# Latents stage rebuilt and run on into the context stage, expert stage's back transposes moved into the first products, row statistics and small attention and last-layer edits

## What is computed

```python
x = x + xattn(ctx_1024, layernorm(x), ...)   # 8192 context rows, 8 heads of 64
x = x + layers(layernorm(x), ...)            # 8 layers: q, k, v, linear attention, MLP 512-2048-512
x = x + experts(layernorm(x), ...)           # 16 experts x 4 sets of 64
```

## Time and profile before

| | us |
|---|---|
| median of 3 runs | 2241.94 |
| lowest and highest | 2238.9, 2242.02 |
| profiled execution | 2242.18 |
| its span in the trace | 2240.4 |

### The profile page before, as it was taken

The page is one execution under the profiler, slowest core; times in us unless marked ns, Lnnn a source line. Parts: engine busy times, 40 slices in busy tenths (PEclk is TensorE's granted clock), DMA queues, the critical chain, the costliest instruction groups (busy, mean ns, idle before and its releaser), DMA issues. The chain is left out here.

```text
span 2240.4 us, 37583 instructions
## 1 busy us (share of the span) xinstructions
PE 2144.8 (96%) x12843; PEld 1082.3 (48%) x12843; DVE 1612.3 (72%) x2356; ACT 1103.8 (49%) x1726; POOL 902.5 (40%) x634
## 2 busy tenths in 40 slices
PE   5899999999999999999899999999999999999976
PEld 2344444433333333333475665757566575756533
DVE  6687777659989999887575757667585666657563
ACT  4122332334444444555464655656474565647445
POOL 0235555559989999600221303122130212213044
PEclk9999999999999999999999999999999999999989
DMA  3345454433322322432323333342333334233313
GB/s 116 130 162 168 167 201 163 148 117 90 93 85 86 97 84 85 124 105 71 125 95 110 98 122 85 132 123 89 114 93 130 85 132 123 81 118 95 116 40 112
DMA packets 159854, 252.75 MB, mean 113 GB/s; under 512 B 11506, under 2 KB 63986, under 8 KB 159730
## 3 DMA queue, kind: packets, MB, share of 16 engines
q1 hardware_dynamic: 159730, 250.96, 35.4%
HBM read 211.73 MB, written 36.70 MB: 111 GB/s over the span
## 5 line engine op out<-in xcount | busy, mean ns | idle before, releaser
L67 PE MATMUL scores<-xt_hi,wt_hi 128*128 128x256 f16 (+3 forms) x1568 | 413.2, 275 | 10.2 <-DVE xt_lo L1418 4.6
L68 PE MATMUL scores<-xt_lo,wt_hi 128*128 128x256 bf16 (+3 forms) x1568 | 413.5, 275 | 0.0
L69 PE MATMUL scores<-xt_hi,wt_lo 128*128 128x256 f16 (+3 forms) x1568 | 413.0, 275 | 0.0
L1375 POOL TENSOR_TENSOR l_rstd<-l_var_eps,neg_half 128x1 f32<-128x1 f32 x71 | 66.6, 938 | 834.6 <-DVE l_var_eps L1429 834.6
L900 DVE TENSOR_REDUCE pmax<-mx 128x1024 f32 (+1 forms) x196 | 239.9, 1224 | 34.5 <-PE mx L1085 22.3
L69 PE MATMUL l_tok<-wt_hi,h_lo 128*128 128x512 f16 x576 | 219.5, 381 | 0.0
L1658 ACT ACTIVATE wt_hi<-stage 128x512 f16<-128x512 f32 x384 | 213.6, 615 | 8.6 <-DMA stage<-in_L_attn_Wf 8.6
L1098 PE MATMUL scores<-q_hi,res 128*128 128x512 f16 x544 | 209.0, 384 | 2.7 <-ACT q_lo L997 1.3
L1099 PE MATMUL scores<-q_lo,res 65*128 65x512 f16 x544 | 207.9, 382 | 0.0
L67 PE MATMUL l_tok<-wt_hi,h_hi 128*128 128x512 f16 x512 | 195.6, 382 | 0.0
L68 PE MATMUL l_tok<-wt_lo,h_hi 128*128 128x512 bf16 x512 | 195.4, 382 | 0.0
(11 more groups left out here) (321 smaller groups left out, 4745.8 us busy)
## 6 DMA issues: line engine op xcount, KB each, us to landing
stage<-in_L_attn_Wf SPq DMA_DIRECT2D x60, 1024.0 KB, 5.2
keys<-wt_hi SPq DMA_DIRECT2D x136, 128.0 KB
res<-keys SPq DMA_DIRECT2D x68, 256.0 KB, 3.3
vb<-values SPq DMA_DIRECT2D x68, 256.0 KB, 5.6
stage<-in_ctx SPq DMA_DIRECT2D x16, 1024.0 KB, 10.0
values<-wt_lo SPq DMA_DIRECT2D x16, 1024.0 KB
stage<-in_L_ffn_f SPq DMA_DIRECT2D x16, 1024.0 KB, 5.3
res<-keys SPq DMA_DIRECT2D x68, 128.0 KB, 5.4
```

The costliest lines, as they stand in the source:

```text
L67: pe.matmul(out, lh, rh, start=first, stop=False, **kw)
L68: pe.matmul(out, lh, rl, start=False, stop=False, **kw)
L69: return pe.matmul(out, ll, rh, start=False, stop=last, **kw)
L1375: g.tensor_tensor(rstd[:, t:t + 1], var_eps[:, t:t + 1], k.neg_half[:, 0:1], ALU.pow).then_inc(rstd_done, 1)
```

## The change

- *Latents.* The two norms become one pass: the inner one's variance is worked out from the outer one's, with two powers on GpSimd and small operations on VectorE. Four banks take the transposes. Wq is loaded ahead of the vectors, and weights are split in four pieces; GpSimd makes the low halves of Wq and of the scaled Wkv. The beta products become `product3`. The statistics of context block 0 stand among the query splits, its normalising among the key splits; its transposes, halves and block 1's statistics move from the context stage into the value products. The value tiles go to `k.res`; SP no longer waits for loads and stores at the end, TensorE, ScalarE and SP do so in the context stage where they need them.
- *Context.* The prologue is gone (counters are raised instead), the two pairs of buffers swap their turns, and in block 0 block 1 is normalised after the second key tile.
- *Attention.* The maxima's two loads are issued ahead of the two value loads; pair 0's sums are cleared by GpSimd; the negated maxima are f16 and meet an f16 identity; `out_copy` comes after the second exponential of a pair.
- *Last layer.* The transposes stand at step 13 of 16.
- *Experts.* The back transposes 4 to 7 go into the third and fourth block of the first product, into the output banks; their copies go to other memory; ScalarE's weight halves 2 and 3 come one block sooner; the second product starts after four copies.

```diff
+        lat_bank = [tp[0][:], tp[1][:], mm[2][:], mm[3][:]]
@@ latents, sync @@
+                sp.dma_start(wq, k.wq.rearrange("(c p) n -> p c n", p=P)).then_inc(wq_in, 16)
                 for n, v in enumerate((k.gamma_x, k.beta_x, k.gamma_l, k.beta_l)):
...
-                sp.wait_ge(km_in, 16 * len(km_rows(0)))
-                sp.wait_ge(stored, 16 * (2 * PAIRS + 1))
-                sp.wait_ge(raw_in, 32)
@@ latents, gpsimd @@
-                for n in range(3):
-                    pool.wait_ge(var_done, n + 1)
-                    g.tensor_tensor(rstd[:], var_eps[:], k.neg_half[:, 0:TT], ALU.pow).then_inc(rstd_done, 1)
+                pool.wait_ge(var_done, 1)
+                g.tensor_tensor(rstd_in[:], var_eps[:], k.neg_half[:, 0:TT], ALU.pow).then_inc(rstd_done, 1)
+                pool.wait_ge(inner, 3)
+                g.tensor_tensor(rstd[:], var_out[:], k.neg_half[:, 0:TT], ALU.pow).then_inc(rstd_done, 1)
+                pool.wait_ge(norm_done, TT)
+                pool.wait_ge(wq_in, 16)
+                for c in range(CH):
+                    pool.wait_ge(w_hi_done, c + 1)
+                    g.tensor_tensor(wq_lo[:, c, :], wq[:, c, :], wq_hi[:, c, :], ALU.subtract).then_inc(wq_lo_done, 1)
+                pool.wait_ge(var_done, 2)
...
+                for c in range(CH):
+                    pool.wait_ge(wg_hi_done, c + 1)
+                    g.tensor_tensor(k.wg_lo[:, c, :], wkv_g[:, c, :], k.wg_hi[:, c, :],
+                                    ALU.subtract).then_inc(wg_lo_done, 1)
@@ latents, vector @@
-                norm(0, k.x_sb, z, EPS_OUTER)
-                norm(1, z, z, EPS_XATTN)
+                v.tensor_tensor(var_out[:], rstd_in[:], rstd_in[:], ALU.mult).then_inc(inner, 1)
...
+                v.tensor_tensor(var_out[:], var_out[:], mv[:, :, 1], ALU.mult).then_inc(inner, 1)
...
+                v.tensor_scalar(var_out[:], var_out[:], EPS_XATTN, None, ALU.add).then_inc(inner, 1)
+                dve.wait_ge(rstd_done, 2)
+                v.tensor_tensor(rstd_in[:], rstd_in[:], rstd[:], ALU.mult).then_inc(inner, 1)
...
+                    if p == 1:
+                        row_stats()
@@ latents, tensor @@
-                        m = t_.matmul(mm[n][:], beta_cols[:, c, :], wkv[:, c, n * D:(n + 1) * D],
-                                      start=c == 0, stop=c == CH - 1)
+                        m = product3(t_, mm[n][:], (beta_hi[:, c, :], beta_lo[:, c, :]),
+                                     (wkv_hi[:, c, n * D:(n + 1) * D], wkv_lo[:, c, n * D:(n + 1) * D]),
+                                     c == 0, c == CH - 1)
...
+                    if t < 2:
+                        row_transposes(t)
+                    if t == 2:
+                        row_transposes(2)
+                        row_transposes(3)
@@ context @@
-                for c in range(CH):
-                    low(0, 0, c)
-                norm_stats(0, 1)
...
-                    if before_end(i, u, 1):
+                    if before_end(i, u, 1) and not is_zero(b):
                         normalise(*after(i, u, 1))
...
+                        if is_zero(b) and tile == 1:
+                            normalise(*after(i, u, 1))
...
-                for c in range(CH):
-                    transposes(0, 0, c)
+                pe.sem_inc(tp_ready, CH)
+                pe.wait_ge(k.lat_km, 16 * len(km_rows(0)))
@@ attention @@
-        rneg = sb("rneg", [P, UNITS], F32)
+        rneg = sb("rneg", [P, UNITS], F16)
...
                 for b in range(2):
+                    load_m(1, b + 2, b)
+                for b in range(2):
                     load_v(0, b, b)
-                for b in range(2):
-                    load_m(1, b + 2, b)
...
+                g.memset(sums[0], 0.0).then_inc(sums_cleared, 1)
...
-                clear_sums(0)
...
-                            if p and b == 0 and j == 0:
+                            if p and b == 0 and j == 1:
                                 out_copy(p - 1)
...
-                                          k.ident[:], start=True, stop=True)
+                                          k.ident16[:], start=True, stop=True)
@@ layers @@
-                            if f == 10 and t:
+                            if f == (13 if last else 10) and t:
@@ experts @@
-        back_late = sel_hi[:, 0:2].rearrange("p c e t s g -> p (c e t s g)").rearrange("p (q t) -> p q t", t=TOK)
+        back_late = wt_hi[:, KQVO + 4:KQVO + 6].rearrange("p a c n -> p (a c) n")
+        back_bank = [work[n % 2] for n in range(QUADS // 4)] + outs
...
                 for b in range(BLOCKS_OF_PAIRS):
                     back_copy(b)
+                    if b == BLOCKS_OF_PAIRS - 1:
+                        back_copy(b + 1)
+                        back_copy(b + 2)
                     act.wait_ge(inner_relu, b + 1)
                     a.activation(in_hi[:, 8 * b:8 * b + 8, :], inner[b % 2], ACT.Copy).then_inc(in_hi_done, 1)
-                    if b >= 2:
-                        weight_high(b)
-                for n in range(QUADS // 4, QUADS // 2):
+                    if b in (1, 2):
+                        weight_high(b + 1)
+                for n in range(QUADS // 4 + 2, QUADS // 2):
                     back_copy(n)
...
-                            back_transposes(b)
+                            for n in ((0,), (1,), (2, 3, 4), (5, 6, 7))[b]:
+                                back_transposes(n)
...
-                for n in range(QUADS // 4, QUADS // 2):
-                    back_transposes(n)
-
...
+                    pe.wait_ge(back_done, q // 2 + 1)
                     pe.wait_ge(it_lo_done, q + 1)
...
-                pe.wait_ge(back_done, QUADS // 2)
+                pe.wait_ge(back_done, QUADS // 4)
```

More of the change, by code:

```diff
@@ L190, in _ @@
+                dve.wait_ge(rstd_done, 2)
+                v.tensor_tensor(rstd_in[:], rstd_in[:], rstd[:], ALU.mult).then_inc(inner, 1)
+                dve.wait_ge(inner, 4)
+                for t in range(TT):
+                    v.tensor_scalar(z[:, t, :], k.x_sb[:, t, :], mv[:, t, 0:1], rstd_in[:, t:t + 1],
+                                    ALU.subtract, ALU.mult).then_inc(norm_done, 1)
                 dve.wait_ge(vec_in, 64)
@@ L203, in _, with row_stats @@
                                     ALU.mult).then_inc(w_scaled, 1)
[L204 to L205 removed]
+                def row_stats():
+                    dve.wait_ge(raw_in, 32)
+                    for t in range(TT):
+                        v.bn_stats(stats[:, t, :], raw[0][:, t, :]).then_inc(stats_done, 1)
+                    dve.wait_ge(stats_done, 2 * TT)
+                    for t in range(TT):
+                        v.bn_aggr(mv[:, t, :], stats[:, t, :]).then_inc(mv_done, 1)
+                    dve.wait_ge(mv_done, 2 * TT)
+                    v.tensor_scalar(var_eps[:], mv[:, :, 1], EPS_XATTN, None, ALU.add).then_inc(var_done, 1)
                 for p in range(PAIRS):
@@ L244, in _ @@
                     a.activation(lat_hi[:, c, :], lat_t[:, c, :], ACT.Copy).then_inc(lat_hi_done, 1)
+                act.wait_ge(wkv_in, 16)
+                for c in range(CH):
+                    a.activation(wkv_hi[:, c, :], wkv[:, c, :], ACT.Copy).then_inc(w_hi_done, 1)
+                act.wait_ge(beta_done, CH)
+                a.activation(beta_hi[:], beta_cols[:], ACT.Copy).then_inc(w_hi_done, 1)
                 for p in range(PAIRS):
@@ L260, in _ @@
                     a.activation(k.kv_bias[:, n * D:(n + 1) * D], mm[n][:], ACT.Copy).then_inc(bias_copied, 1)
+                for c in range(CH):
+                    act.wait_ge(tp_ready, CH + c + 1)
+                    a.activation(k.f_hi[:, c, :], tp[c % 2][:], ACT.Copy).then_inc(lat_hi_done, 1)
             @block.tensor
@@ L623, in key_high @@
                     act.wait_ge(k_added, 4 * (2 * i + u) + tile + 1)
+                    if is_first(i) and u == 1 and tile == 0:
+                        act.wait_ge(k.lat_stored, 16 * (2 * PAIRS + 1))
                     if not is_first(i) and tile == 0:
@@ L635, in values @@
                                  ACT.Copy).then_inc(v_copied, 1)
-                for c in range(CH):
-                    high(0, 0, c)
+                act.sem_inc(xt_hi_done, CH)
                 def body(i, u):
```

181 lines of the change are left out of this document (113 added, 68 removed).

## The result

The changed kernel takes 2218.51 us (median; 2217.54 to 2220.97) against 2241.98 for the kernel before on the same chip: ratio 0.9907, 95% interval 0.9893 to 0.9921, 23.5 us saved. Measured a second time it took 2218.12 us, ratio 0.990 (0.9885 to 0.9914). The prediction was 2213.6 in a range from 2206 to 2221: sign and range hold, but 28.3 us were promised and about 5 of them are missing. The profiled execution is the longest of its four, 2220.97 (span 2219.2), so its trace has 21.2 us to show against the 2242.18 before; that of the second measurement took 2218.08, close to its median, and has 24.1. I give both.

The account below looks back on a forecast made before the run. TensorE, busy 96% of the span, was taken as the bound, with gains only where it starts late or stops. Savings of 14.0 + 0 + 5.4 + 6.0 + 2.9 = 28.3 off the 2241.94 median gave 2213.6 us, range 2206 to 2221.

Parts of the forecast that it names:

- The front: Latents stage up to the first context key product: 14.0 us saved, that product at about 64.9.
- the seam: Between latents and context stage: 1.9 us in place of 4.70, 2.8 saved.
- Start 1.3: Attention's start: ScalarE's clearing goes, 0.5 us, and one-pass f16 row matmuls save 0.8.
- 0 saved: Context block 0: old stall and clock loss of 4.3 us go, a late table costs 4.3; from -3.5 to +3.
- the 0.5 of clearing: Attention's start: ScalarE no longer clears ahead of the negated maxima, 0.5 us saved.
- Pair changes: Attention, three pair changes: shorter f16 rows save 2.8 us, TensorE's vanished waits for an exponential 1.3.
- the third rival: Attention gives nothing: GpSimd's sums set the pace, the 4.1 us at pair changes are lost; 2217.7, chance 3%.
- Last layer and experts: Last layer: later transposes bring the last bias 6.0 us sooner; experts: slot 4's weights 2.9 us sooner, ScalarE as bound.
- Rivals 1 and 2: Rival 1 as on its own line; rival 2: table early, ScalarE not expert bound, clock steady, 2205.6 or less, 8%.
- rival 1: Part is returned: table lands after 8.7, VectorE waits for GpSimd in full, expert chain stays; 2223, chance 14%.
- Rivals 3 and 4: Rival 3 is the third rival; rival 4: attention edits do not do what they say, 2219.0, 3%.
- rival 5: Slower: short TensorE stops in the layers drop its clock, 1.7 us a fall, 17 falls needed; chance 2%.

## Why the prediction was right and where it failed

**The front was right, to a tenth, and partly by luck.** Transposes came at 13.37 instead of 12.95, since the last tile of x landed later (why was not tried); two subtractions met GpSimd and took 1.16 and 0.92 us instead of 0.62, where 1.3 more were set aside for up to three; the next ones, after GpSimd had finished at 18.25, took 0.67 and 0.69. Each of the two ended 0.54 or 0.55 us behind the end of the GpSimd operation that was running. So they waited for the rest of one operation, and not for a whole one each. Bias product, row transposes, the seam with 1.90 us of idle time and the 5.4 us of prologue all came as priced.

**The failed step is the one of one sentence: "The maxima's loads ahead of the value loads: nothing, with 2 us either way".** It cost 3.5 to 3.9 us by the medians of the run that takes it back and 3.8 by the ratio of the run that makes it alone. The same part of the prediction says that TensorE starts earlier, by shorter clearing and rows, and the new order puts two other loads ahead of one that TensorE soon asks for. The two loads and their dates had to be set side by side, as I did for the table: issue of the first value load, a landing, and the time at which the first weighted values ask for it.

**"Start 1.3" failed in part as well.** The rows came earlier by 0.5 and are shorter by 1.3 (0.40 against 1.71), but the next thing is late then, the key load, which ends a wait of 2.10 us where 1.33 had been ScalarE's. And with the value loads first again, pair 0 is 1.7 us longer than before where a gain of 0.8 was forecast: the first maxima load is 1.47 late there, and the clock falls behind that stop. Pair 0 came to -5.3 and -4.1 where +0.8 stood in the sum, 6.1 and 4.9 less; the order is 3.6 of the one and 2.4 of the other (151.26 less 148.87), not all.

**Block 0 was "0 saved" and came to -2.2 and -2.6** (the table's -1.7 and -2.1 less the 0.5 of clearing), inside its -3.5 to +3. In the profiled run its losses are 3.57 for the first stop, 1.7 for the clock and 1.22 for the second stop, 6.5 together, where the prediction had 2.3, 0.8 and 1.2. So the mis-sized terms are the table's landing (7.0 us for 5.2) and the clock, taken at half. The 1.2 behind normalising came true by luck: the pass was priced at 1.91 and took 4.20, since the edit put it beside GpSimd's turn, but the longer first stop hid most of that. With the table early it shows, as 3.16.

**Pair changes: right in sum (4.1 against 4.6), wrong in parts.** The pairs became shorter by 1.20, 1.48 and 1.88 us, 4.6 together. With the other edit kept, undoing the f16 rows costs 2.1 (0.53, 0.52 and 1.08) and undoing the copy's place 0.9. So either edit by itself would bring more than half of the 4.6, and the second adds less: TensorE then reaches VectorE's maxima too early at the first two pair changes. That is a piece of the third rival, with VectorE where it had GpSimd, and worth half a microsecond a pair and not the 4.1 that it claimed.

**Last layer and experts were right in mechanism and a little small.** VectorE's cycle of 12.05 us was 11.95 (2112.69 less 2100.74 in its timeline), so 6.7 instead of 6.0 on the path; the layers ahead of it gave another 0.8 that I had not claimed and did not look into. Slot 4's weights stand 43.0 us behind the first expert product instead of 47.5, 4.4 nearer where 2.9 were forecast; in the two traces of the changed kernel 2.0 and 3.7 of it reach the end. Layers and experts, 2.2 over their forecast in the second trace, hid a part of the miss.

Rivals 1 and 2 did not come true: the table's late landing, a part of rival 1, happened, GpSimd's full waits and the fixed expert chain did not. Rivals 3 and 4 name times (2217.7 and 2219.0) that are nearer to the 2218.5 than the forecast, but not for their reasons: the pair changes gave 4.6 us, and the rows fell to 0.40 us. The clock (rival 5) did fall one more time, at the attention's start, behind the stop of 3.38 us; in the layers it did not.

## What to carry to other kernels

When a change makes a consumer start earlier and also reorders the loads in front of it, write for each load its issue, its landing and the date of its first use; the load that is used first is issued first, and an edit that "only reorders" is priced like a wait. And try repairs of neighbouring stops together: in block 0 they brought the rows 1.5 and 3.1 us forward alone and 6.5 as a pair, while at the pair changes two gains on the same engine run into the same next limit, and together they give less than their two single gains added up.

## What the runs showed of the hardware that I had not expected

- VectorE's pass with one SBUF input, normalising 128x512 in f32, is held up by GpSimd as the subtraction with two inputs is: four take 1.91 us alone (0.48 each) and 4.20 beside GpSimd's turn. In the latents stage, one alone beside a GpSimd subtraction:

```profile
41.22 2.12 POOL L175 TENSOR_TENSOR wt_lo<-wt_hi 128x1024 bf16<-128x1024 f32 x1 [0.46 <-ACT wt_hi L315]
41.56 2.06 DVE L255 TENSOR_SCALAR stage<-stage,mv,rstd 128x512 f32<-128x512 f32 x1
```

  It ends 0.28 us behind GpSimd's end (43.34), and so do the others of this pass, and the first three in block 0, to within 0.01. Subtractions with one input in PSUM were 0.68 to 0.69 us in the same stretch, as always. The Trainium skill (SBUF — State Buffer, Who interferes with whom) says that tensor_scalar in its two-port mode takes the shared pair of ports for the whole instruction and the other engine waits; the trace agrees, with GpSimd as the one that holds the pair, and by it the moved pass could have been priced: each operation waits for the rest of the GpSimd operation that is running.
- Issuing the same four loads on SyncE took 7.1 us with the maxima loads first (3.19 and 3.87 for two each; 7.0 in the kernel before with that order) and 4.2 with the value loads first (1.57 and 2.55), while a single one of each takes 0.52 and 0.40 later in the stage. Why the order matters for the issue was not tried.
- A stop of 3.4 us behind another one was followed by 1.8 us more in the next eight f32 matmuls (1.97 and 1.92 us for four instead of 1.08 and 1.03), at the lower clock. The length of a stop alone doesn't tell it: in block 0, with the table early, TensorE stopped for 3.16 us and the granted clock stayed at 1.00 (76 to 85), while behind stops of 2.81, 3.56 and 3.57 us there it fell, and at the attention's start one of 1.47 us was enough.
